# TensorE's other work in a state-space scan, divided into halves and put behind each half of a state's feed

## The reference, cut to what matters

```python
u2  = silu(causal_conv(u) + conv_b)
dt  = softplus(dt_low @ W_dt + b_dt)
A   = -exp(A_log)
def step(h, inp):                       # over 512 tokens, for each of 4 batches
    dA = exp(dt_t[:, :, None] * A)
    h  = dA * h + (dt_t * u_t)[:, :, None] * B_t[:, None, :]
    y  = einsum('bdn,bn->bd', h, C_t)
y   = ys + u2 * D
out = (y * silu(z)) @ W_out
...
x   = x + x1 + out
```

## Time and profile before

| | |
|---|---|
| three executions | 1572.98 us median (1572.09 to 1573.34) |
| the profiled execution | 1575.7 us, span 1573.9 us |
| busy in the span | TensorE 1439.2 us (91%), VectorE 1068.6 us, ScalarE 855.6 us, GpSimd 477.6 us |
| the scan stage | 321.4 to 647.0 us from the span's start |

### The profile page before, as it was taken

How to read it: one execution, slowest core, us unless ns; L and a number is a source line. 1 busy time by engine, 2 the same in 40 slices (tenths; PEclk the granted TensorE clock), 3 DMA queues, 4 the chain that set the end, 5 groups by cost and what they waited for, 6 DMA issues and landing times.

```text
span 1573.9 us, 20191 instructions
## 1 busy us (share of the span) xinstructions
PE 1439.2 (91%) x7404; PEld 984.9 (63%) x7404; DVE 1068.6 (68%) x1218; ACT 855.6 (54%) x1509; POOL 477.6 (30%) x140
## 2 busy tenths in 40 slices
PE   5798798589998999998998889999989999999997
PEld 3576343389797979743444333333358888888886
DVE  5997395789989899863443567777563565565655
ACT  2443456599899988631343177777632533333332
POOL 0999120079888888400331320000000000000000
PEclk7899999789999999988999999999999999999999
DMA  7110010501323211401102132443000000000000
GB/s 268 23 65 1 1 54 2 202 28 69 121 81 134 81 54 41 165 15 27 58 23 83 49 94 57 132 140 94 1 1 0 1 14 1 1 14 1 14 1 14
DMA packets 36624, 87.61 MB, mean 56 GB/s; under 512 B 8350, under 2 KB 24948, under 8 KB 32948
## 3 DMA queue, kind: packets, MB, share of 16 engines
q1 hardware_dynamic: 36532, 86.39, 16.2%
HBM read 68.10 MB, written 18.21 MB: 55 GB/s over the span
## 4 chain that ended last, share of the span: by engine, by line
PE 71%; ACT 10%; DVE 9%; DVEq 5%; issue 3%; POOL 1%; DMA 1%; ACTq 0%; SPq 0%
PE ps L1442 12%; PE ps L1451 12%; PE ps L1008 5%; PE ps L1310 4%; PE ps L1383 4%; PE ps L1177 4%; PE ps L993 3%; ACT arena L1730 3%; DVE arena L2034 3%; ACT arena L1718 3%; PE ps L1298 2%; DVEq L2033 2%; PE ps L994 2%; PE ps L1026 2%; PE ps L1203 2%
## 5 line engine op out<-in xcount | busy, mean ns | idle before, releaser
L2596 POOL TENSOR_TENSOR arena<-arena 128x2048 f32<-128x2048 f32 x63 | 287.6, 4584 | 150.5 <-DVE arena L2134 150.1
L2134 DVE TENSOR_TENSOR_SCAN arena<-arena,ps 128x1024 f32<-128x1024 f32 x128 | 284.4, 2272 | 32.4 <-issue 16.1
L1730 ACT ACTIVATE arena<-arena,mam 128x511 f32<-128x511 f32 x256 | 166.7, 721 | 25.6 <-DVE arena L2134 25.5
L1911 ACT ACTIVATE arena<-ps,rho 128x512 f32<-128x512 f32 x256 | 158.6, 690 | 30.9 <-PE ps L1383 29.6
L2368 DVE TENSOR_REDUCE mxs<-ps 128x1 f32<-128x512 f32 x224 | 140.7, 684 | 43.3 <-PE ps L1298 41.5
L993 PE MATMUL ps<-early,arena 128*128 128x128 f32 x768 | 129.9, 278 | 15.0 <-DVE arena L2134 13.3
L1940 ACT ACTIVATE arena<-arena 128x256 f32<-128x256 f32 x192 | 85.8, 503 | 81.3 <-DVE arena L2539 50.2
L1442 PE MATMUL ps<-early,arena 128*128 128x256 f32 x512 | 127.1, 380 | 2.9 <-DVE mam L2535 1.8
L2576 POOL TENSOR_TENSOR arena<-arena 128x4096 f32<-128x4096 f32 x16 | 115.0, 7189 | 43.7 <-DVE arena L2053 43.7
L1718 ACT ACTIVATE arena<-arena,early 128x512 f32<-128x512 f32 x192 | 124.7, 720 | 4.4 <-DVE arena L2112 4.4
L1451 PE MATMUL ps<-arena 128*128 128x256 f32 x512 | 121.0, 379 | 1.2 <-issue 1.2
(11 more groups left out here) (349 smaller groups left out, 2483.5 us busy)
## 6 DMA issues: line engine op xcount, KB each, us to landing
arena<-bc_scratch SPq DMA_DIRECT2D x32, 512.0 KB, 3.7
arena<-in_ffn SPq DMA_DIRECT2D x8, 1024.0 KB, 4.9
batch_scratch<-arena SPq DMA_DIRECT2D x2, 3072.0 KB, 8.8
arena<-batch_scratch SPq DMA_DIRECT2D x6, 1024.0 KB, 6.7
arena<-q_scratch SPq DMA_DIRECT2D x96, 64.0 KB, 2.2
arena<-k_scratch SPq DMA_DIRECT2D x96, 64.0 KB, 2.2
arena<-in_dec_w SPq DMA_DIRECT2D x1, 3855.0 KB, 16.5
arena<-in_cond SPq DMA_DIRECT2D x1, 3739.5 KB, 11.5
```

The source lines that it names most:

```text
L1730: last = act.activation(decay[:, (2 * k + h) % 3, i, 1:S], dt[b % 2][:, m, 1:S], ACT.Exp, scale=a_neg[:, m * NS + n:m * NS + n + 1])
L1911: act.activation(pt[:, j % 4, i], ps[:, 3 + (hg + n) % 3, :], ACT.Exp, scale=rho[:, 0:1]).then_inc(s_pt, 1)
L2134: dve.tensor_tensor_scan(half, view(decay[:, (2 * k + h) % 3], [[1, 2 * S]]), view(ps[:, FEED + 2 * h, :], [[1, 2 * S]]), 0.0, ALU.mult, A ...
L2596: pool.tensor_tensor(state[:, k % SLOTS], state[:, k % SLOTS], view(c_rows[:, j % 2, k % G, :], [[0, M], [1, S]]), ALU.mult).then_inc(s_hc, 1)
```

## The change

TensorE's work between two steps' feeds (sums, D term, output projection) stood in one piece behind both halves of a feed. Now it is cut into halves, and one stands behind each half of the feed. A sum is cut by token tiles: tiles 2 and 3 first (behind `feed(k, 1)`, they wait for GpSimd), tiles 0 and 1 behind the next feed half. `mamba_out` is cut into its two pairs of matmuls; the first pair waits only for ScalarE's copy, the second only for VectorE's. State 5 takes two whole sums in place of one. The sums owed are made up for at up to two half sums behind a feed half. On VectorE, `residual(b-1, 0)` moves from between the two scans of state 4 to ahead of them.

```diff
-            def d_term(b, n):
+            def d_term(b, n, h):
...
-                for m in range(M // 2 * (n % 2), M // 2 * (n % 2 + 1)):
+                t, m = (n - D_FROM) // 2, 2 * (n % 2) + h
...
-            def sum_state(k):
-                if k < B * NS - 1:
-                    pe.wait_ge(s_hc, k + 1)
+            def sum_half(unit):
+                k = unit // 2
+                if unit % 2 == 0:
+                    if k < B * NS - 1:
+                        pe.wait_ge(s_hc, k + 1)
+                    else:
+                        pe.wait_ge(s_ends, 2)
+                    sum_tiles(k, (2, 3))
                 else:
-                    pe.wait_ge(s_ends, 2)
-                sum_tiles(k, range(TILES)).then_inc(s_y, 1)
+                    sum_tiles(k, (0, 1)).then_inc(s_y, 1)
...
+            def mamba_half(b, o, bank, half):
                 if o == 0:
-                    pe.wait_ge(s_g01, b + 1)
-                    pe.wait_ge(s_g23, b + 1)
+                    pe.wait_ge(s_g23 if half else s_g01, b + 1)
...
-                feed(k, 0)
-                feed(k, 1)
-                if b and n == 2:
-                    turn_back(b - 1)
-                elif b and n == 3:
-                    mamba_out(b - 1, 0, 0)
-                elif b and n == 4:
-                    mamba_out(b - 1, 1, 1)
-                elif b and n == 5:
-                    pe.wait_ge(s_hc, due + 1)
-                    sum_tiles(due, (2, 3))
-                    pe.wait_ge(s_x1, C * b + 1)
-                    sum_tiles(due, (0, 1)).then_inc(s_y, 1)
-                    due += 1
-                else:
-                    for _ in range(2):
-                        if due <= k - 2:
-                            sum_state(due)
-                            due += 1
+                for h in range(2):
+                    feed(k, h)
+                    ready = 2 * (k - 2 + h)
+                    if b and n == 2:
+                        if h:
+                            turn_back(b - 1)
+                    elif b and n in (3, 4):
+                        mamba_half(b - 1, n - 3, n - 3, h)
+                    elif b and n == 5:
+                        if h:
+                            pe.wait_ge(s_x1, C * b + 1)
+                        sum_half(due + h)
+                        sum_half(due + h + 2)
+                        due += 4 * h
+                    else:
+                        at_end = n < 2 or k >= B * NS - 2
+                        for _ in range(4 if at_end else 2 if ready - due > 2 else 1):
+                            if due < ready:
+                                sum_half(due)
+                                due += 1
                     if n >= D_FROM:
-                        d_term(b, n)
+                        d_term(b, n, h)
...
-                if b and n == 5:
-                    residual(b - 1, 1)
+                if b and n in (4, 5):
+                    residual(b - 1, n - 4)
                 scan(k, 0)
-                if b and n == 4:
-                    residual(b - 1, 0)
                 scan(k, 1)
```

More of the change, by code:

```diff
@@ L947, in turn_du @@
                     last.then_inc(s_duT_mm, 1)
-            def d_term(b, n):
-                if b >= 2 and n == D_FROM:
+            def d_term(b, n, h):
+                if b >= 2 and n == D_FROM and h == 0:
                     pe.wait_ge(s_back_u2, 16 * (b - 1))
-                for m in range(M // 2 * (n % 2), M // 2 * (n % 2 + 1)):
[L953 to L956, removed]
+                t, m = (n - D_FROM) // 2, 2 * (n % 2) + h
+                last = pe.matmul(ps[:, t, m * P:(m + 1) * P], u2[b % 2][:, m, t * P:(t + 1) * P], diag[:, m, :],
+                                 start=False, stop=False, skip_group_check=True)
+                if n == NS - 1 and h == 1:
                     last.then_inc(s_dterm, 1)
@@ L1018, in turn_back, with mamba_out @@
                 last.then_inc(s_g_turned, 1)
-            def mamba_out(b, o, bank):
+            def mamba_half(b, o, bank, half):
                 if o == 0:
-                    pe.wait_ge(s_g01, b + 1)
-                    pe.wait_ge(s_g23, b + 1)
+                    pe.wait_ge(s_g23 if half else s_g01, b + 1)
                 g = view(zT[b], [[S, M], [1, S]])
-                for m in range(M):
+                for m in (2 * half, 2 * half + 1):
                     last = pe.matmul(ps[:, bank, :], w_out[:, m, o * P:(o + 1) * P], g[:, m, :],
                                      start=(m == 0), stop=(m == M - 1))
-                last.then_inc(s_out_mm, 1)
+                if half:
+                    last.then_inc(s_out_mm, 1)
+            def mamba_out(b, o, bank):
+                mamba_half(b, o, bank, 0)
+                mamba_half(b, o, bank, 1)
             due = 0
@@ L1080, in _ @@
             last.then_inc(s_prep_mm, 1)
-            sum_state(due)
-            sum_state(due + 1)
+            assert due == 2 * (B * NS - 2)
+            for unit in range(due, 2 * B * NS):
+                sum_half(unit)
             pe.wait_ge(s_scan, 2 * B * NS)
```

## The result

| | before | after |
|---|---|---|
| executions beside each other | 1572.98 us median (1572.04 to 1576.12, 5 runs) | 1580.24 us median (1578.86 to 1580.62, 5 runs) |
| the same two kernels once more | 1574.34 us (1572.21 to 1580.42, 21 runs) | 1579.35 us (1577.07 to 1583.03, 9 runs) |
| the profiled execution | 1575.7 us, span 1573.9 | 1578.9 us, span 1577.0 |

The changed kernel takes 1.0036 times as long (95% interval 1.0022 to 1.0049), and 1.0030 (1.0016 to 1.0044) the second time: slower by 5 to 7 us, where I had forecast 1 us faster and a range that ended at 1576.4. The prediction was wrong.

What follows compares the result with a forecast made beforehand. In the scan TensorE's feeds and sums and VectorE's scans wait for each other in turn. Order of work -2.7 plus clock +1.7 gives -1.0 us: median 1572.98 to 1572.0, range 1568.8 to 1576.4.

Steps and rivals of the forecast that it cites:

- the sum for the order: Scan stage: all effects of reordering TensorE's work, clock left out, over all batches: -2.7 us.
- State 3: Second half feed now stands behind the wait for ScalarE's copy and a projection pair, lengthening the chain: +1.10 us.
- States 5 to 8: TensorE-bound states: two sums in state 5 cost +1.76; the next three gain -0.84, -0.86 and -1.77 us.
- State 9 to state 1: Into the next batch: scans back to back, three pauses of 0.38 go (-1.14), less 0.44 lost: -0.7 us.
- State 0's +0.44: Three half sums instead of two keep TensorE busy 4.84 us, so the next feed comes 0.44 us late.
- Batch 3: VectorE carries `linear_weights` steps between scans from state 6 on, busy in the pauses to be removed: only -0.3 us.
- Batch 0: Runs at ScalarE's pace, 4.60 us a state, which stays: no gain.
- the second rival: ScalarE or GpSimd bounds states 9 to 17 and takes the gain: 1574.5 us; chance 0.14.
- with nothing at all in it I expect three in three: +1.7: TensorE's emptied wait before the first projection: clock drops in three of three batches instead of two, 1.70 us each.
- the rival on the slower side: Longer wait before the projection costs more than one low-clock stretch each time: +4.1 us, 1577.1; chance 0.13.
- No oftener a fall than before: Clock drops no more often at batch turns, so the reordering's -2.7 stands alone: 1570.3 us; chance 0.22.
- The change does all that its shape suggests: A third of VectorE's 32.4 idle us ahead of scans goes, 10.8: 1562.2 us; chance 0.06.

Runs made afterwards that it cites:

- the filled kernel: Changed kernel plus eight unused transposes in state 3 ahead of the wait for ScalarE's copy, where the half feed stood: 1573.03 us, 0.9974 of the kernel before.
- the first experiment's kernel: Changed kernel with only state 3 as before: the whole first output projection behind both half feeds again; 1570.68 us, 0.9956 of the kernel before.
- h1_state0: Changed kernel with state 3 as before the change and state 0's half sums spread, without unused transposes: 1568.33 us, 0.9953 of the kernel before.

## Why the prediction was wrong

**What bounds the kernel, and the order of work: right.** With the clock taken out, the stage is 321.94 in the old order and 327.55 - 1.07 - 7.48 = 319.0 in the new one; the filled kernel gives the same, 320.70 - 1.70. That is -2.9 where the sum for the order was -2.7. By its terms:

- State 3, forecast +1.10 a turn: 12.73 - 11.63 = 1.10. Its scan's wait was forecast at 414.9 - 412.7 = 2.2, and is 2.17 once the clock holds.
- States 5 to 8, forecast 1.76 - 0.84 - 0.86 - 1.77 = -1.71: 26.31 - 28.04 = -1.73. TensorE's states are 5.71, 5.71, 4.82 and 4.41 apart, as in the forecast.
- State 9 to state 1, forecast -0.7: -0.88. Two pauses of about 0.36 are left, ahead of 442.89 and 482.92. State 0's +0.44 is real: spreading its half sums gives back 0.47 in 9-2 and 0.26 in 0-2.
- Batch 3, forecast -0.3: 1.10 - 1.16 = -0.06.
- Batch 0, forecast 0, and state 0 of batch 1: -0.3 and +0.4. The clock also fell once in batch 0 in two of after's three profiles (0.65 over 328 to 332), at no cost that shows: 73.29, 73.29 and 73.28 to batch 1's first scan.
- ScalarE and GpSimd kept up, so the second rival is out. ScalarE's idle time ahead of decays fell from 25.6 to 17.2, more than the 2 to 3 I gave. GpSimd ran ten in a row at 45.23/10 = 4.52:

```profile
447.47 45.23 POOL L2603 TENSOR_TENSOR arena<-arena 128x2048 f32<-128x2048 f32 x10 [0.30 <-DVE arena L2143]
```

**The step that failed is the clock's: "with nothing at all in it I expect three in three: +1.7".** The count was right, three in three. Both other parts of that term were wrong.

The price of a fall. I took 1.70 from the row of a half-busy lull. In batches 1 and 3 the clock fell within the empty lull, 1.1 and 0.7 us before the projection started, and stayed low for 6.9 and 6.8 us, not 3.4. Three falls cost 7.48, not 5.1. This is the mechanism of the rival on the slower side ("the clock stays low for twice as long"), which got 0.13; it had them long in all three batches, four falls' worth more than before, and they were long in two: 7.5 - 3.4 = 4.1 us more, 2.4 falls' worth.

The base. I subtracted the two falls of before's profiled execution, 3.4 us, and wrote that it stood above the median by something "of which the change touches nothing". Against that execution the scan's sum is now -2.9 + 7.5 - 3.4 = +1.2; against an execution with no fall it is +4.6. (Profile against profile the scan stage lost 2.06 - 1.07 = 1.0.) Measured were 7.3 and 5.0. So the wrong price turns the forecast's sign, and it comes near the measured loss of the second comparison only if most executions of before have no fall, which the runs leave undecided (below).

The Trainium skill, "TensorE: Matmul & The Clock Gate", section "Why this matters for your kernels", says that an idle gap between bursts of matmuls brings the clock back to its lower level. The trace agrees for empty lulls: 12 falls in 12.

**The other rivals.** No oftener a fall than before (0.22): refuted, three in three in each of three profiles. The change does all that its shape suggests (0.06): VectorE's idle time ahead of scans is 32.2, not a third less.

**What stays open.** It is open how many falls at the turns an unprofiled execution of before has. Its mean clocks of 0.963 and 0.964 say only that many had less of the lower level in all than any profile of it, and the changed kernel's lay at 0.953 to 0.959 in all 14 timed executions. It is open, too, whether the change costs something in the stages behind the scan. They took 928.65, 928.76 and 928.73 in the three profiles of after, and 927.0, 925.5 and 931.0 in the three of before. The same code ranged from 925.35 to 931.01 over all profiles, in step with the clock there, so what remains is whether the change brings falls there: the first experiment's kernel, with the same order but for state 3, had 927.1, and `h1_state0`'s 930.0. Three of each don't tell a cost of 1 or 2 us from chance. Both bear on the same few us between the shown +1.2 to +4.6 and the measured 5.0 to 7.3. Why a fall is long is known only as far as when it starts: the six long ones began 0.7 to 1.1 us before the projection, the six short ones behind an empty lull between 0.2 before and 0.2 behind its start, with the same idle 3.02 us ahead. What sets that moment no run shows.

## What to carry to other kernels

Before moving an instruction behind a wait, look at what it does where it stands: here a half feed of 1.10 us in a lull of 3 was worth more as a part of what keeps TensorE's clock up (4.1 to 7.5 us over three turns) than as a feed (3.3), and the halving of sums, freed of that one move, is worth 0.4 to 0.5%. Where a cost comes and goes from turn to turn, a single profile says neither how often it comes nor, if the lull grows, what it will cost; profile the kernel before several times and set the sum against its full-clock time.

## What the runs showed of the hardware

- Eight transposes of 128x128, 1.05 us in all, behind a half feed kept the granted clock at 1.00 through the lull: no fall in 12 turns, against 6 in 15 with the half feed alone. Alone in the lull they did it twice in three.
- The clock's lower level came in two lengths behind one and the same idle gap of 3.02 us: 3.4 us at a price of 1.70, and 6.8 to 6.9 us at 2.81 and 2.97. It was long in the six turns where it began 0.7 us or more before the work did, and short in the six others.
- Ahead of the very first scan VectorE waited 7.33 or 6.26 us with no edit near it, as the clock was at its lower level for the first feed (first group 0.90 us) or not (0.55).
- Unchanged code behind the scan took 925.4 to 931.0 us over 14 profiles, in step with 35 to 50 us at the clock's lower level.
